# Cross-attention context taken with its channels first: no transposes on TensorE, the split into high and low parts on ScalarE and GpSimd

## What is computed

```python
def _L0_xattn_ref(x, cond, mask, wq, bq, wk, bk, wv, bv, wo, bo):
    q = _w8a8_linear(x, wq, bq).reshape(B, N, H, D).transpose(0, 2, 1, 3)
    k = (cond @ wk.T + bk).reshape(B, L, H, D).transpose(0, 2, 1, 3)
    v = (cond @ wv.T + bv).reshape(B, L, H, D).transpose(0, 2, 1, 3)
    scores = jnp.einsum('bhnd,bhld->bhnl', q, k) * inv_sqrt_d + mask[:, None]
    attn = jax.nn.softmax(scores, axis=-1)
    o = jnp.einsum('bhnl,bhld->bhnd', attn, v)
    o = o.transpose(0, 2, 1, 3).reshape(B, N, C)
    return _w8a8_linear(o, wo, bo)
```

## Time and profile before

| | |
|---|---|
| device time, median of 3 | 944.49 us (940.9 to 945.22) |
| device time of the profiled execution | 937.71 us |
| its span, first to last instruction | 936.0 us |
| mean granted TensorE clock | 0.94 |
| self-attention | 0 to 76 us |
| `FIRST` | 76 to 128 us |
| 15 batches with a projection beside them | 128 to 807 us |
| last batch, then feed-forward | 807 to 858, 858 to 936 us |
| ACT busy, DVE busy, POOL busy | 555.3, 569.6, 71.3 us |

### The profile page before, as it was taken

One profiled execution on the slowest core, in us unless ns is written; L12 is line 12 of the kernel. 1 busy time (PEld: TensorE's weight loads), 2 busy tenths in 40 slices (PEclk: granted clock), 3 DMA queues, 4 the chain that ended last, 5 costly groups with the idle time before them and its releaser, 6 DMA issues. The chain is left out here.

```text
span 936.0 us, 19297 instructions
## 1 busy us (share of the span) xinstructions
PE 805.2 (86%) x7771; PEld 675.9 (72%) x7771; DVE 569.6 (61%) x1090; ACT 555.3 (59%) x945; POOL 71.3 (8%) x84
## 2 busy tenths in 40 slices
PE   4945689989999999999999999999999989848855
PEld 3533478777877887778787878788888878726644
DVE  3795466656665566565746665666556656636746
ACT  2513156767676667676767676677767775624423
POOL 1021000000000000000000000000000000061633
PEclk8965799999999999999999999999999999977978
DMA  6009566675757575757676667676767674560231
GB/s 180 14 20 279 142 141 170 151 186 131 185 131 179 131 179 137 172 144 164 151 158 151 159 158 167 161 160 165 164 160 162 164 165 95 122 173 8 83 96 40
DMA packets 70279, 133.34 MB, mean 142 GB/s; under 512 B 24112, under 2 KB 53464, under 8 KB 70104
## 3 DMA queue, kind: packets, MB, share of 16 engines
q1 hardware_dynamic: 66016, 123.39, 55.5%
q0 software_dynamic: 2048, 7.34, 2.9%
q10 hardware_dynamic: 2128, 1.38, 0.5%
HBM read 52.59 MB, written 5.57 MB: 62 GB/s over the span
## 5 line engine op out<-in xcount | busy, mean ns | idle before, releaser
L1296 ACT ACTIVATE probsT<-ps_T 125x448 f32<-125x448 f32 x376 | 191.6, 545 | 171.4 <-PE ps_T L1168 156.6
L1398 DVE CUSTOM_DVE_ANT_0 scores<-ps_scores,mask_sb 112x1500 f32<-112x1500 f32 x128 | 219.7, 1717 | 71.7 <-PE ps_scores L1146 64.2
L1168 PE MATMUL ps_T<-ident,scores 112*128 112x112 f32 (+1 forms) x1536 | 196.2, 264 | 25.0 <-ACT probsT L1296 23.0
L1168 PEld LDWEIGHTS ps_T<-ident,scores 112*128 112x128 f32 (+1 forms) x1536 | 173.8, 147 | 52.6 <-ACT probsT L1296 31.6
L1284 ACT ACTIVATE scores<-scores,shift 112x1500 f32<-112x1500 f32 x128 | 197.3, 1542 | 2.7 <-issue 2.1
L1134 PE MATMUL ps_proj<-wkvT,room 128*125 128x256 f32 x1152 | 158.8, 287 | 7.1 <-DVE v_sb L1376 7.0
L1126 PE MATMUL ps_proj<-room,wkvT 128*128 128x500 f32 x576 | 159.2, 413 | 4.0 <-DVE room L1381 3.3
L1134 PEld LDWEIGHTS ps_proj<-wkvT,room 128*125 128x125 f32 x1152 | 145.4, 187 | 16.0 <-DVE v_sb L1376 7.2
L1385 DVE SCALAR_TENSOR_TENSOR room<-ps_proj,xbk,room 128x500 fp32r<-128x500 f32 x96 | 70.8, 738 | 105.0 <-ACT room L1279 104.8
L1146 PE MATMUL ps_scores<-k_stack,q_stack 96*112 96x500 f32 x384 | 118.0, 415 | 6.7 <-DVE shift L1398 6.1
L1126 PEld LDWEIGHTS ps_proj<-room,wkvT 128*128 128x128 f32 x576 | 104.7, 195 | 26.2 <-issue 5.2
(11 more groups left out here) (257 smaller groups left out, 569.8 us busy)
## 6 DMA issues: line engine op xcount, KB each, us to landing
k_stack<-room SPq DMA_DIRECT2D x384, 187.5 KB, 4.0
ctx_rows<-in_ctx SPq DMA_DIRECT2D x48, 500.0 KB
mask_sb<-in_mask_BxSxS_ff SPq DMA_DIRECT2D x32, 328.1 KB
q_stack<-q_hi SPq DMA_DIRECT2D x32, 112.0 KB, 5.6
q_hi<-k_stack SPq DMA_DIRECT2D x4, 448.0 KB, 3.8
q_lo<-k_stack SPq DMA_DIRECT2D x4, 448.0 KB, 4.0
q_stack<-q_lo SPq DMA_DIRECT2D x16, 112.0 KB, 5.5
x_sb<-in_x SPq DMA_DIRECT2D x1, 896.0 KB, 6.4
```

Source lines behind the costliest of these rows:

```text
L1168: last = nc.tensor.transpose(ps_T[0:wide, (TB * t + k) % 2, j * PN:(j + 1) * PN], scores[:, t % 2, key:key + wide], keep["ident"][0:PN, 0:PN])
L1296: nc.scalar.activation(probsT[:, t % 2, k * TC:(k + 1) * TC], ps_T[0:LT, (TB * t + k) % 2, 0:TC * PN].rearrange("p (j n) -> p j n", j=TC), ...
L1398: nc.vector.tensor_tensor_reduce(out=split(scores[:, t % 2], NC), in0=ps_scores[0:PN, :, 0:LC], in1=split(mask_sb[:, a], NC), scale=-1.0, ...
```

## The change

The context comes into the kernel with its channels first (16 x 256 x 1500; the transposition lies outside the timed program), and is loaded as 128 channels x 2 halves x 500 rows for a chunk. The six X units are gone: `split_hi` on ACT copies a whole chunk (128x2x500) from SBUF to `cT_hi`, and `split_context` on POOL subtracts for `cT_lo`; for batch 0 DVE subtracts. A chunk of `cT_hi` may be written when the last K or V unit that reads it has run (`readers_done`). SP reloads a chunk's buffer when its low part is made. The remaining twelve units stand one in each slot.

```diff
 def load_chunk(sp, io, keep, b, c):
-    sp.dma_start(split(keep["context"][0:LT], NL)[:, c * TC:(c + 1) * TC],
-                 io["ctx"][b, c * LC:(c + 1) * LC].rearrange("(j p) d -> p j d", p=LT)).then_inc(keep["ctx_in"][c], 16)
+    sp.dma_start(context_of(keep)[:, :, c * LC:(c + 1) * LC],
+                 io["ctxT"][b, :, c * LC:(c + 1) * LC].rearrange("(m p) l -> p m l", p=P)).then_inc(keep["ctx_in"][c], 16)
 UNITS = [
-    ([("X", 0, 0), ("X", 0, 1)], [("X", 1, 0), ("X", 1, 1)], [("X", 2, 0), ("V", 0, 0), ("X", 2, 1)]),
-    ([("K", 0, 0)], [("K", 0, 1)], [("K", 0, 2), ("V", 1, 0)]),
-    ([("V", 2, 0)], [("V", 3, 0)], [("V", 4, 0)]),
-    ([("K", 1, 0)], [("K", 1, 1)], [("K", 1, 2), ("V", 5, 0)]),
+    ([("V", 0, 0)], [("V", 1, 0)], [("V", 2, 0)]),
+    ([("K", 0, 0)], [("K", 0, 1)], [("K", 0, 2)]),
+    ([("V", 3, 0)], [("V", 4, 0)], [("V", 5, 0)]),
+    ([("K", 1, 0)], [("K", 1, 1)], [("K", 1, 2)]),
 ]
-FIRST = [("X", 0, 0), ("X", 0, 1), ("K", 0, 0), ("X", 1, 0), ("X", 1, 1), ("K", 0, 1), ("X", 2, 0), ("X", 2, 1), ("K", 0, 2),
-         ("V", 0, 0), ("V", 1, 0), ("V", 2, 0), ("V", 3, 0), ("K", 1, 0), ("K", 1, 1), ("K", 1, 2), ("V", 4, 0), ("V", 5, 0)]
+FIRST = [("K", 0, 0), ("K", 0, 1), ("K", 0, 2), ("V", 0, 0), ("V", 1, 0), ("V", 2, 0), ("V", 3, 0),
+         ("K", 1, 0), ("K", 1, 1), ("K", 1, 2), ("V", 4, 0), ("V", 5, 0)]
+def chunk_of(u):
+    kind, p, q = u
+    return q if kind == "K" else (2 * p + 1) // TC
 # SP, in batch()
-                                sp.wait_ge(unit_in_psum, first + at[("X", c, 1)] + 1)
+                                sp.wait_ge(ctx_lo, NC * (b + 1) + c + 1)
                                 load_chunk(sp, io, keep, b + 2, c)
 # GpSimd
+                def split_context(b):
+                    for c in range(NC):
+                        e = slice(c * LC, (c + 1) * LC)
+                        pool.wait_ge(ctx_in[c], 16 * (b + 1))
+                        pool.wait_ge(unit_in_psum, readers_done(b, c))
+                        pool.wait_ge(ctx_hi, NC * b + c + 1)
+                        nc.gpsimd.tensor_tensor(cT_lo[:, :, e], context[:, :, e], cT_hi[:, :, e].bitcast(F32), ALU.subtract).then_inc(ctx_lo, 1)
 # TensorE, in unit()
+                    pe.wait_ge(ctx_lo, NC * n + chunk_of(u) + 1)
 # ScalarE
+                def split_hi(b, c):
+                    e = slice(c * LC, (c + 1) * LC)
+                    act.wait_ge(ctx_in[c], 16 * (b + 1))
+                    if b > 0:
+                        act.wait_ge(unit_in_psum, readers_done(b, c))
+                    nc.scalar.activation(cT_hi[:, :, e], context[:, :, e], ACT.Copy).then_inc(ctx_hi, 1)
 # ScalarE, in batch()
                         units_hi(d, 0)
+                        if project and d == 0:
+                            split_hi(b + 1, 1)
                         probs_out(2 * d + 1)
                         next_exponentials(2 * d)
                         units_hi(d, 1)
+                        if project and d == 0:
+                            split_hi(b + 1, 2)
                         next_exponentials(2 * d + 1)
                         units_hi(d, 2)
+                        if b + 2 < B and d == DUOS - 1:
+                            split_hi(b + 2, 0)
                     act.wait_ge(values_done, (b + 1) * NP + 2)
                     nc.scalar.activation(keep["outT"][:, a], ps_out[:, 0:DUOS * PN], ACT.Copy).then_inc(out_copied, 1)
```

More of the change, by code:

```diff
@@ L606, in projection_room, with last_reader @@
     k_hi, k_lo = (room[:, 2 * n + k * L:2 * n + (k + 1) * L] for k in range(2))
-    context = split(keep["context"][0:LT], NL)
-    return cT_hi, cT_lo, k_hi, k_lo, context
+    return cT_hi, cT_lo, k_hi, k_lo, context_of(keep)
+def chunk_of(u):
+    kind, p, q = u
+    return q if kind == "K" else (2 * p + 1) // TC
+def last_reader(at, c):
+    return max(n for u, n in at.items() if u[0] in "KV" and chunk_of(u) == c)
 def expert_room(keep):
@@ L947, in cross_attention_phase @@
         out_copied = sem("out_copied")
-        load = {n: sem(f"in_{n}") for n in ("wo", "w", "gate", "atom_w", "atoms", "imp", "bo", "bv")}
+        load = {n: sem(f"in_{n}") for n in ("wo", "w", "gate", "atom_w", "atoms", "imp", "bias")}
         ones_set = sem("ones_set")
@@ L1113, in unit @@
                         return
-                    if kind == "X":
-                        if q == 0:
-                            pe.wait_ge(ctx_in[p], 16 * (n + 1))
-                        for j in range(TC):
-                            last = nc.tensor.transpose(ps_proj[:, bank, j * LT:(j + 1) * LT],
-                                                       context[:, p * TC + j, q * P:(q + 1) * P], keep["ident"][0:LT, 0:LT])
-                    elif kind == "K":
-                        pe.wait_ge(unit_out, first + at[("X", q, 1)] + 1 + 2)
+                    pe.wait_ge(ctx_lo, NC * n + chunk_of(u) + 1)
+                    if kind == "K":
                         c, e = slice(q * LC, (q + 1) * LC), slice(p * P, (p + 1) * P)
@@ L1347, in prepare @@
                         nc.scalar.activation(keep["w_stack"][0:E], gate, ACT.Copy).then_inc(w8_hi_ready, 1)
+                for c in range(NC):
+                    split_hi(0, c)
                 for n, u in enumerate(FIRST):
```

72 lines of the change are left out of this document (41 added, 31 removed).

## The result

The changed kernel takes 910.3 us (median of 4 runs, 903.7 to 926.0) against 942.7 for the kernel before in the same session; the ratio is 0.963, 95% interval 0.955 to 0.971. Two later sessions gave 0.976 (0.965 to 0.986) and 0.966 (0.959 to 0.973). So it is faster, by 32 us between the medians and 35 by the ratio; I had forecast 896, inside a range of 864 to 926. Some executions (here the one of 926.0) are slower at a lower clock whatever the kernel: medians are of all runs, ratios and their intervals of the others alone, and where such a one was profiled, the table of the experiments has no entry in its last two columns. The profiled execution took 914.05 us, where my sum gave 889.2.

A forecast was written before the change was run, and what follows sets the result against it. PE's order bounds the kernel, with the K stack's DMA loop right beside. Batches -39.5 and start -9 give -48.5 us: the profiled 937.7 becomes 889.2, as a median 896 us, own range 880 to 912, wider range 864 to 926.

The forecast's parts named there:

- The chain at the border: From a batch's last K hi: ACT's copy, then POOL's subtraction; V 0 after 4.0 us, next K hi after 15.2, with R 17.0.
- The middle: Last K hi of K 0 to first of K 1: released by the stack's DMAs after 14.2 us, R costing nothing.
- 15 batches: Each batch with a projection takes 41.8 us, with R 43.6; 639.6 in all against 679.1, so -39.5 us.
- the first rival: Both hand-overs, border and middle, cost less than taken: 38.0 or 40.8 us a batch, 846 us in all; chance 0.17.
- The start: Before the batches: gate table stored 3 us earlier, with 6 us less waiting for its landing; -9 us, bounds 0 and -12.
- The last batch and the feed-forward: The kernel's end, after the batches with a projection: no change there, so 0 us.
- ACT's queue at the border: ACT's outT and first copies queue 1.0 us behind split_hi; would put V 0 at 2.9 us, inside the 4.0, costing nothing.
- another longest wait: Sign of being wrong: PE's longest wait is not the one put down to POOL, between a last K hi and V 0.
- POOL's lock on DVE: POOL's three 2.3 us subtractions a batch may hold DVE; exposed only the small R chain in 7 batches, at most 32 us.
- the third rival: POOL's subtractions hold DVE's masks and read-outs: 1000 us if all stood before them; chance of slower by it 0.04.
- The second rival: Context loads still reach into or collide with the stack; K 0 to K 1 stays 16.5 us, 930 us total; chance 0.15.

The follow-up runs named there:

- the second one: The changed kernel run once more, unchanged, against the kernel before: 915.2 us, ratio 0.976 (0.965 to 0.986).
- another kernel: Against the changed kernel, GpSimd also makes chunk 0's high part from batch 1 on, removing ACT's split_hi at the border: 871.8 us, ratio 0.928 to the kernel before.

## Why the prediction was right, and where it was off

The time lay in the range and the sign was right, but less of it came from the batches than I had said: they gave 12.4 us of the forecast 39.5 in this execution and 22.8 in the second one. That the total still lay in the range is partly luck: the range was wide, and 7.7 of the 23.7 us between the profiled executions come from the last batch, where I had forecast nothing. Its own steps against the profiled execution, 914.05 us, 24.9 over my 889.2 (27.1 from the 15 batches, 3.7 from the start, -7.7 from the last batch, 1.8 from the feed-forward):

- **The chain at the border.** V 0 4.0 us after the last K hi, border 15.2: measured 4.2 and 15.3. Right, at the full clock. With R I took 1.8 more; at the full clock it is 1.5 (16.8 for 17.0). But in this execution all seven borders with R had a dip and took 18.2 us or more, and the first took 19.9: the mean was 17.3 us, where my prices make it 16.0.
- **The middle.** 14.2 us, released by the stack: measured 14.3 to 15.6, mean 14.7. The mechanism is right, the size 0.5 short, about 7 us in 15 batches. The 16.5 us from which I started was that of one batch; the mean before the change was 15.7.
- **15 batches**, 639.6 us: measured 789.18 - 122.51 = 666.7. This is the step that failed, by 27 us. I let PE stand 2.4 us at each border and priced the wait alone. In the runs such waits also lower the granted clock, and the matmuls behind them take longer (12 of them 2.77 us instead of 1.66). Of the 27 us, 19 lie at the borders and 7 in the middles. With the waits filled the 14 batches come back from 621.8 us to 600.1, against 597.8 by my prices. The middle's 0.5 is in there, partly paid by R's smaller price. That a cheaper hand-over is worth much, the thought of the first rival, showed only in another kernel: taking the chain away gave 43 us.
- **The start**, -9 us: the first probabilities came at 122.5 instead of 127.9, so -5.3. I took 4 us for the landing of the gate store; it took SP 9.1. The new loads are gone sooner but were still ahead of it, and in the run with the table first its 4.1 us were lost again with the stack.
- **The last batch and the feed-forward**, 0: 43.4 us instead of 51.1 from the end of batch 14 to that of batch 15. I can't put these 7.7 us down to the change: the changed kernel again and the one with idle matmuls, with the same instructions there, took 43.4 and 49.4 us, and on the next chip all four kernels took 32.6 to 34.8, whatever was changed. They hid a quarter of the error, which is luck. What makes that batch so variable stays open.
- **ACT's queue at the border.** I had `outT` and the first copies 1.0 us late behind `split_hi` at no cost. PE's longest wait turned out to be that for ACT's copies of `probsT` (31.5 us between 128 and 770, against 15.1 for POOL), at the border and at K 1,1; I had named another longest wait as a sign that I was wrong, and this one came. By the border's 15.3 us it adds nothing to the chain, as I had it, but it is the other half of the idle stretch that the clock answers to.
- **POOL's lock on DVE.** Masks took 1.72 us as before. Of the small R chain, the addition of line 838 took 0.89 us beside POOL (0.41 before the change), as the third rival allowed; DVE is not the limit there. The run with DVE making the low parts gained too; its chain was 1.2 us shorter at each border.
- **The second rival** (the DMA loop stays where it was) didn't happen. That the spread of the loads is the reason is borne out by the run with 125 + 3 rows, in which the whole gain is gone and the middle is back at its mean of before, 15.7 us, though that run also has twice as many loads. The rival's price was too high: 1.0 us a middle, not 2.3.
